# A second buffer for the gate-weight rows that VectorE ranks in a mixture-of-experts stage

## The reference, cut to what matters

```python
probs = softmax(xf @ gate_w.T + gate_b)          # 625 tokens x 8 experts
topw, topi = top_k(probs, 2)
wm = where(routed, w_te, -1.0)                   # gate weight, or -1
sel_w, sel_idx = top_k(wm.T, cap)                # cap = 93 tokens for each expert
h = gelu(xf[sel_idx] @ w1 + b1)                  # 512 -> 2048
out = h @ w2 + b2                                # 2048 -> 512
of = zeros.at[sel_idx].add(out * max(sel_w, 0))
```

## Time and profile before

| what | value |
|---|---|
| median of 3 runs | 2194.7 us (2192.68 to 2194.94) |
| the profiled execution, its own time | 2190.48 us |
| span of the profiled execution (first to last instruction) | 2188.6 us |
| TensorE busy | 2114.8 us, 97% |
| VectorE busy | 1507.9 us, 69% |
| ScalarE busy | 1123.9 us, 51% |
| the mixture of experts, first `up` to the last combine | about 214 to 482 us |

### The profile page before, as it was taken

One profiled execution on the slowest core, in us unless ns is written; L12 is line 12 of the kernel. 1 busy time (PEld: TensorE's weight loads), 2 busy tenths in 40 slices (PEclk: granted clock), 3 DMA queues, 4 the chain that ended last, 5 costly groups with the idle time before them and its releaser, 6 DMA issues.

```text
span 2188.6 us, 36234 instructions
## 1 busy us (share of the span) xinstructions
PE 2114.8 (97%) x13402; PEld 1968.5 (90%) x13402; DVE 1507.9 (69%) x3184; ACT 1123.9 (51%) x3011; POOL 855.9 (39%) x687
## 2 busy tenths in 40 slices
PE   8887799999899999999999999999999999999998
PEld 7766566669779999999999999999999999999997
DVE  8737689854456767677776767777676676767676
ACT  4534556632455554455555445555554555555454
POOL 0000000000145555455555544555554455555461
PEclk9888899999999999999999999999999999999999
DMA  6000688871021231111122111112221111231110
GB/s 212 1 20 5 222 280 277 279 261 32 9 82 62 86 99 63 62 62 62 63 85 99 64 62 62 62 62 83 101 64 62 63 62 62 81 102 65 59 44 24
DMA packets 85688, 197.44 MB, mean 90 GB/s; under 512 B 5937, under 2 KB 10321, under 8 KB 85511
## 3 DMA queue, kind: packets, MB, share of 16 engines
q1 hardware_dynamic: 85512, 195.12, 26.5%
HBM read 193.75 MB, written 1.35 MB: 89 GB/s over the span
## 4 chain that ended last, share of the span: by engine, by line
PE 89%; ACT 4%; DVE 4%; DMA 1%; issue 1%; POOL 1%; SPq 0%; DVEq 0%; POOLq 0%; ACTq 0%
PE PS L54 80%; PE PS L53 5%; PE PS L57 3%; ACT HW L88 1%; ACT GT L88 1%; DMA WB<-w_rows 1%; DMA X<-in_x 0%; ACT HS L88 0%; DVE SM L107 0%; POOL SM L60 0%; DVE OHs L68 0%; DVE JU L66 0%; DVE M L75 0%; DVE OHd L69 0%; DVE SM L75 0%
## 5 line engine op out<-in xcount | busy, mean ns | idle before, releaser
L54 PE MATMUL PS<-ZH,WS 128*128 128x314 f32 x4096 | 946.4, 311 | 0.0
L54 PEld LDWEIGHTS PS<-ZH,WS 128*128 128x128 f32 x4096 | 692.2, 189 | 0.0
L54 PE MATMUL PS<-ZL,WS 128*128 128x314 f32 x2048 | 626.1, 306 | 0.0
L60 DVE TENSOR_TENSOR ACC<-ACC,PS 128x314 f32<-128x314 f32 x1008 | 476.4, 477 | 196.7 <-PE PS L54 186.8
L54 PEld LDWEIGHTS PS<-ZL,WS 128*128 128x128 f32 x2048 | 387.7, 189 | 0.0
L60 POOL TENSOR_TENSOR WS<-RAW,WS 128x512 fp32r<-128x512 f32 x256 | 326.5, 1296 | 116.6 <-ACT WS L88 116.6
L60 POOL TENSOR_TENSOR ZS<-ZS,ZQ 128x628 f32<-128x628 f32 x128 | 198.4, 1550 | 230.7 <-ACT ZQ L88 230.4
L60 POOL TENSOR_TENSOR ML<-MF,MH 128x400 fp32r<-128x400 f32 x124 | 130.9, 1056 | 363.6 <-ACT MH L88 363.6
L88 ACT ACTIVATE ZH<-PS,g1T 128x628 fp32r<-128x628 f32 x128 | 100.5, 785 | 313.5 <-PE PS L54 313.5
L88 ACT ACTIVATE EE<-EE,SM 125x100 f32<-125x100 f32 x640 | 233.0, 376 | 0.1
L88 ACT ACTIVATE MF<-PS 128x400 f32<-128x400 f32 x128 | 64.7, 506 | 315.8 <-PE PS L53 315.8
(11 more groups left out here) (338 smaller groups left out, 3731.3 us busy)
## 6 DMA issues: line engine op xcount, KB each, us to landing
RAW<-in_L_ffn_wz_w SPq DMA_DIRECT2D x66, 1024.0 KB, 6.0
RAW<-in_L_ffn_w SPq DMA_DIRECT2D x64, 1024.0 KB, 7.6
RAW<-in_L_ffn_Wq_w SPq DMA_DIRECT2D x32, 1024.0 KB, 8.5
CB<-c_rows SPq DMA_DIRECT2D x32, 195.3 KB
RAW<-in_L_gnn_W SPq DMA_DIRECT2D x4, 1024.0 KB, 8.9
RAW<-in_L_ffn_Wkv_w SPq DMA_DIRECT2D x4, 1024.0 KB, 5.4
RAW<-in_L_ffn_Wk_T SPq DMA_DIRECT2D x2, 1024.0 KB, 5.3
WB<-w_rows SPq DMA_DIRECT2D x6, 305.2 KB
```

The lines of the kernel that those rows point to most:

```text
L54: return self.q.matmul(o, l, r, start=start, stop=stop)
L60: return Nothing() if self.q is None else self.q.tensor_tensor(out=o, in0=a, in1=b, op=op)
```

## The change

There are two tiles, `WB[0]` where `WB` was, and `WB[1]` at the address of `WMT`. Expert e uses `WB[e % 2]`, so `load_row(e)` now waits for the rank of expert e-2, and each buffer's loads have a semaphore of their own. Row 2 is loaded directly after the write of `w_rows` has landed, ahead of the loop over the chunks; row 3 stands where row 2 stood (after load 2), and after the loads with m % 8 == 6 stands row m//8 + 4. Since `WB[1]` lies on `WMT`, the two copies of expert 1's row wait for the write of `w_rows` instead of for the rank of expert 0.

```diff
-        WB = at("WB", [P, 625], f32, after("io94"))
-        JU = at("JU", [P, 2, 626], f16, after("WB"))
+        WB = [at("WB0", [P, 625], f32, after("io94")), at("WB1", [P, 625], f32, after("LT8"))]
+        JU = at("JU", [P, 2, 626], f16, after("WB0"))
...
             def load_row(e):
-                q.wait_ge(*rank_v.of(e - 1, "sum"))
-                q.dma(WB[:, :], wrow[e:e + 1, :].broadcast_to([P, 625])).then_inc(s_wrow, 16)
+                q.wait_ge(*rank_v.of(e - 2, "sum"))
+                q.dma(WB[e % 2][:, :], wrow[e:e + 1, :].broadcast_to([P, 625])).then_inc(s_wb[e % 2], 16)
...
             q.wait_ge(s_wrow, 16)
+            load_row(2)
             for m in range(64):
                 q.wait_ge(*w_used.of(m))
                 load(q, N_MOE + 8 + m)
                 if m == 2:
-                    load_row(2)
+                    load_row(3)
...
-                if m % 8 == 6 and m // 8 + 3 < NE:
-                    load_row(m // 8 + 3)
+                if m % 8 == 6 and m // 8 + 4 < NE:
+                    load_row(m // 8 + 4)
...
             def rank_row(e):
                 q.wait_ge(*row_mm.of(e))
                 if e:
-                    q.wait_ge(*rank_v.of(e - 1, "sum"))
-                q.act(WB[:, 0:500], PS[0:P, 4, 0:500], ACT.Copy).then_inc(*row_done.up(e))
+                    q.wait_ge(s_wrow, 16)
+                q.act(WB[e][:, 0:500], PS[0:P, 4, 0:500], ACT.Copy).then_inc(*row_done.up(e))
...
-                    q.wait_ge(s_wrow, 16 * e)
+                    q.wait_ge(s_wb[k], 16 * (e // 2))
```

More of the change, by code:

```diff
@@ L1001, in program @@
         w_hi, w_lo, w_used, s_wrow = count("w_hi"), count("w_lo"), count("w_used"), sem("s_wrow")
+        s_wb = [sem(f"s_wb{k}") for k in range(2)]
         row_mm, row_done, rank_v = count("row_mm"), count("row_done"), count("rank_v")
@@ L1302, in rank_tiles @@
                     if t:
-                        q.ts(JU[:, 0, 0:n], WB[:, 0:n], w, None, ALU.is_ge, ALU.add, acc=rk[k][:, t:t + 1])
-                    q.ts(JU[:, 0, n:625], WB[:, n:625], w, None, ALU.is_gt, ALU.add, acc=rk[k][:, 5 + t:6 + t])
-                    q.stt(JU[:, 1, 0:P], WB[:, n:n + P], w, BIGM[:, :], ALU.is_equal, ALU.mult, acc=rk[k][:, 10 + t:11 + t]).then_inc(*rank_v.up(e, t, "eq"))
+                        q.ts(JU[:, 0, 0:n], WB[k][:, 0:n], w, None, ALU.is_ge, ALU.add, acc=rk[k][:, t:t + 1])
+                    q.ts(JU[:, 0, n:625], WB[k][:, n:625], w, None, ALU.is_gt, ALU.add, acc=rk[k][:, 5 + t:6 + t])
+                    q.stt(JU[:, 1, 0:P], WB[k][:, n:n + P], w, BIGM[:, :], ALU.is_equal, ALU.mult, acc=rk[k][:, 10 + t:11 + t]).then_inc(*rank_v.up(e, t, "eq"))
             def rank_end(e):
@@ L1320, in row_tail @@
                 if e:
-                    q.wait_ge(*rank_v.of(e - 1, "sum"))
-                q.cp(WB[:, 500:625], PS[0:P, 5, 0:P]).then_inc(*rank_v.up(e, "tail"))
+                    q.wait_ge(s_wrow, 16)
+                q.cp(WB[e][:, 500:625], PS[0:P, 5, 0:P]).then_inc(*rank_v.up(e, "tail"))
             def dispatch(e):
```

## The result

The changed kernel takes 2180.14 us in the median of 4 runs, the kernel before 2194.82 (4 runs): 14.7 us less. The ratio of the two sets of runs is given as 0.9945 (95% interval 0.9934 to 0.9957), which is 9.4 to 14.5 us; the quotient of the two medians, 0.9933, lies just outside it. Two later measurements of the same kernel gave ratios of 0.9954 (0.9942 to 0.9966) and 0.9957 (0.9943 to 0.9971), 9.9 and 9.4 us less in the medians. The forecast was 13.3. The mean of all 14 executions of the changed kernel is 2183.0 us, that of all 61 of the kernel before is 2193.5, so that 10.5 us is the better figure for what the change is worth. Two executions of far more than 2200 us, one of the kernel before (2977.55) and one of the kernel with rows and bias spread (5323.64), are left out of every median, mean and ratio here.

A forecast was written before the change was run, and what follows sets the result against it. It took the file TensorE, ScalarE, VectorE within an expert as the bound, plus one wait for row 2's transfer. Terms of 10.81, 2.35 and 0.11 us sum to 13.27: 2194.7 - 13.3 = 2181.4 us, range 2177.5 to 2186.5.

The forecast's parts named there:

- the case that was given a chance of 0.80: Whole kernel: the stall in expert 0 goes and the full 13.3 us, give or take 1.5, are gained; chance 0.80.
- The case given 0.12: Experts 0 and 1: the DMA engines become the bound, gain 10.9 us, 2183.8 us; chance 0.12.
- Term 1, the stall: In dispatch(1), TensorE goes on 10.81 us earlier without the wait for row 2.
- Term 2, the clock: The 16 matmuls after the stall run at clock 1.00, not 0.50: 2.82 us instead of 5.17, gain 2.35.
- Term 3: From the end of those matmuls to the next `HS` copy: 18.21 us instead of 18.32, gain 0.11.
- Row 2 in time: Row 2, issued at about 206.9, lands by 220.7 at worst, wanted at 227.16: 6.5 us of slack, no cost.
- added waits: ScalarE's `rank_row(1)` and VectorE's `row_tail(1)`, the latter at 212.16, wait for the `w_rows` write issued at 201.93: no cost.
- moved transfers: Row 3 in row 2's old place leaves the queue unchanged from 219 to 238 us; lands around 239, wanted at 259.1.
- What is late next: Chunks after the stall: load 3 has 1.0 us of slack, load 10 is 1.0 late but hidden; cost 0, bounds 0 and 2.4.
- The rival of the DMA engines: In experts 0 and 1, load 3 lands later by one row's 3.4 us and 2.4 us come back; chance 0.12.

The follow-up runs named there:

- rows and bias spread: The changed kernel with each row broadcast to 128 partitions instead of 125 and the bias to 96 instead of 94: 2180.79 us, 0.9950 against the kernel before.
- The filled stall: The kernel before with 46 matmuls put into TensorE's idle time in dispatch(1), VectorE's wait kept: 2190.08 us, ratio 0.9982.

## Why the prediction was right or wrong

The median of 2180.14 us lies 1.3 us from the forecast, but in part by luck: the stage gave 9.0 to 10.8 us where 13.3 were forecast, and the case that was given a chance of 0.80 (the full 13.3 us, give or take 1.5) is not what happened in any of the three profiles. The case given 0.12, that the DMA engines take part of it back (gain 10.9, 2183.8 us), is; the two later medians are 2184.68 and 2184.44.

*Term 1, the stall.* Right. TensorE went on 10.91 us after expert 0's copy, before 21.76: 10.85 against a forecast of 10.81. (The "some 20 us" read off the chain's 1% were too many; the transfer in it is the 13.75 us of the earlier trace rows.)

*Term 2, the clock.* Right, 5.17 to 2.81 us, 2.36 against 2.35. The filled stall shows it by itself.

*Term 3.* 18.32 to 18.20, 0.12 against 0.11.

*Row 2 in time, added waits, moved transfers.* Right as far as expert 0 goes. Row 2 was through 3.5 us after its issue. The two buffers without the early load are worth nothing either way, so the waits for the write cost nothing.

*What is late next.* This step failed. "Two chunks matter" named loads 3 and 10. Load 3 wasn't waited for; it landed 1.1 us before its copy, 1.0 forecast. Load 10 was late, by 2.4, 0.6 and 0 us in the three profiles where I had 1.0, and hidden as said. But load 9, which I didn't look at, had the least slack of all: before, it landed at 266.97 + 7.9 = 274.87, and its copy started at 274.90. I set its landing among the distances and never against its use. By my own prices it would have landed at 241.5 + 6 x 2.6 + 3.4 + 2.6 = 263.1, and its copy would have started at 274.90 - 13.27 = 261.6: 1.5 us late. Two prices were also too low. The bias, taken like a row at 3.4 us, costs 4.8 (load 2's landing with and without it spread). The five small loads got the price of one chunk in the queue and nothing in SyncE's list, where they hold load 9 back by 2.4 us. And I had no term for what a new idle gap of TensorE does to its clock, though term 2 had just priced it. In place of the 0 that I took stand 3.3, 2.5 and 4.3 us in the three profiles, of which 1.8, 1.0 and 1.1 are added idle time of TensorE in dispatch(2) and dispatch(3); the rest goes with the halved clock behind it.

*The rival of the DMA engines.* What it said came true, at another place and by another path: not load 3 in expert 0, but load 9 in expert 1. Its 2.4 us were near the size.

*The sum.* On the stage 9.0 to 10.8 us of the 13.4 that a kernel without late chunks gains (109.14 - 95.76). That the first median showed 14.7 us is then not a larger effect; the three medians, 9.4 to 14.7, scatter around what the profiles show and around the 10.5 us of the means. In the profiles the scatter arises before the stage, where expert 0's copy comes 220.6 to 226.9 us after the start; what causes it there is open. The range held because it reached to the late chunks.

## What to carry to other kernels

A wait that occurs once in a pipeline is removed by moving one transfer to where its queue is empty; look for the earliest such place before adding a buffer, and check what the buffer is for. When a stall is removed, go through all loads of the next periods, each landing against its use: the one with the least slack sets what comes back, and small transfers count with the time that their issue holds the queue's engine. Broadcasts to 94 or 125 partitions are worth padding when chunks stand behind them: 96 for 94 took the three experts from 98.3 to 100.1 us down to 95.96, and 128 for 125 on top of it to 95.76.

The version to take is the changed kernel with rows and bias spread: no late chunk is left, the three experts take 95.8 us, and with 20 matmuls ahead of dispatch(0) its median was 2179.2 us, the lowest measured, if not clearly under the changed kernel's 2180.1 to 2184.7. The cheapest version is the one line that moves row 2's load behind load 0, with one buffer: 99.4 us for the three experts.

## What the runs showed of the hardware

- An issue by SyncE is not always short. The same 4 KB load took 0.64 to 0.95 us to issue in the three kernels with rows and bias spread, 2.90 with the bias alone spread, 2.90 to 3.48 in the four where the stall or the late row held expert 0 back, and 5.15 to 5.39 in the changed kernel.
- The bias of 188 KB on 94 partitions weighed more on the queue than the row of 305 KB on 125. Spreading it brought the landing of the chunk right behind it from 10.5 to 5.7 us; spreading the row brought the chunk behind the row from 8.5 to 7.7.
- TensorE's clock is at a cliff in dispatch(1) to dispatch(3). After 0.72 to 0.99 us of idle time there it stayed at 1.00 in every profile. After 1.36, 1.60, 1.85, 1.90, 1.99, 2.12 and 2.92 us it fell to 0.50 somewhere in the matmuls behind, and after 2.06 us, in one execution, it didn't. A full fall costs 2.4 us, twice the wait that leads to it.
